# First block's norm, transposes and logits one step later, and the second group's tile numbers loaded behind a second layer's products

## The chip, the cores and the metric

The kernel runs on one core of a Trainium2 chip. The metric is the device time of one execution in microseconds; three runs of the kernel before have a median of 201.23 us (200.9 to 202.34). The engines are TensorE (PE, with its weight loads as PEld), VectorE (DVE), ScalarE (ACT), GpSimd (POOL) and SyncE (SP), which here only issues transfers. Each engine takes its instructions in order, and they wait for one another through semaphores.

## The reference

The input is 8 sequences of 256 tokens with 128 features. Two mixtures of experts run one after the other, and their result is added to the input.

```python
# stage 1, per sequence: two of eight experts, chosen from cond_8, and a shared one (inner width 512)
w, sel = top_k(softmax(cond), 2); w = w / w.sum()
c = sum_e w_e * ((gelu(x @ g_e) * (x @ u_e)) @ d_e) + (gelu(x @ sg) * (x @ su)) @ sd
# stage 2, per token: one of eight experts, and a shared one (inner width 256), weights rounded to three levels
h = layernorm(c) * gamma + beta
probs = softmax(h @ router_w.T)
ffn = silu(h @ sw1.T) @ sw2.T + max(probs) * (silu(h @ ew1[argmax].T) @ ew2[argmax].T)
out = x + ffn
```

## The kernel before

**Stage 1** is a loop over steps. A step is one sequence, one expert and one half of its inner width. The 16 shared steps come first, then 32 steps for the chosen experts, numbered (i, q) with i from 0 to 3 and q from 0 to 7: two sequences for each i, four steps for each sequence. In a step TensorE makes the gate product and the up product (`gate_up`, lines 446 to 448, 12 matmuls of 256 columns, since 16-bit high and low parts stand for 32-bit values), and the down product of the step three before (`down`, lines 473 to 475, 6 matmuls). ACT makes the gelu (line 728) and the high part of the product of the step before (`act_part_hi`, line 734); DVE makes the product (line 906) and its low part (line 912). There are two banks for gate and up each, so the gate/up product of a step waits until gelu and product of two steps earlier are done.

**Between the steps** the preparation of stage 2 is interleaved, at places that tables name by (i, q). For a block of four tiles of 128 tokens (two sequences) it runs: `to_tokens` (TensorE transposes the result of stage 1 into the bank ps_a, line 493), `statistics` (DVE), `deviation` (POOL, lines 1281 and 1283, gives `rstd` and `shift`), `normalise` (ACT, line 774, reads ps_a and writes `norm`), `to_features` (TensorE transposes `norm` into the bank ps_b, line 500), `features` (ACT, line 781), `logits` (TensorE, line 507, into ps_b) and `choose` (DVE, lines 993 to 1002, reads ps_b). The tables are TOKENS_AT, NORM_AT, FEATURES_AT and LOGITS_AT; the first entry of each is that of the first block. `abs_sums(f)` (ACT, lines 761 and 763) and POOL's `round_first` round the first-layer weights of expert f; `round_second` does it on DVE for the second layer, and `second_weights(k)` transposes two of these on TensorE (line 519) into ps_b, from where ACT copies them (line 769). A wait guards each use of ps_a and ps_b. Within a step TensorE does `gate_up`, then what the tables put there, then `down`. ACT does gelu, the high part of the step before, `abs_sums`, `second_weights`, `normalise`, `features`, in this order.

**Stage 2** has units: three shared ones, eight tile units (TU[0] to TU[7], of 3 or 4 tiles of tokens that a scatter through device memory has sorted by expert; four for the first group of tokens, four for the second), one shared and four dense ones. For each unit TensorE makes the first layer (`first_layer`, lines 624, 630, 639), ACT the silu (lines 836 to 846), TensorE the second layer (`second_layer`, line 664), and DVE takes the result. The loop runs first_layer(u), sorted_T for unit u + 2 (transposes of its sorted tokens, line 594), second_layer(u - 1). The weights of a tile unit are addressed by registers of TensorE's sequencer. `experts_of(g)` (line 601) waits for the table of group g and loads its tile numbers into these registers, 15 for group 0 and 13 for group 1, with one TENSOR_LOAD. Group 1 is needed from TU[4] on.

## Time and profile before

| | |
|---|---|
| median of three runs | 201.23 us |
| the profiled execution | 203.34 us, of which the span from first to last instruction 201.6 us |
| busy: PE, DVE, ACT, POOL | 169.7, 136.8, 114.6, 86.3 us |
| mean granted clock of TensorE | 0.947 of 2.4 GHz |

Read the rows as follows. A timeline row has the start in us, the duration in us, the engine, the line of the kernel, the operation with its output and input, a count, and in brackets how long the engine had been idle before and who ended that. A merged row lasts from its first to its last instruction. A windows row has the stretch, its length, the engine's busy time in it with the number of instructions, the granted clock of TensorE as a share of 2.4 GHz, the busy share of the DMA engines and GB/s. A waits row names who waited for whom, with the total in us, how many times, and the longest. Durations in the view of one line are in ns. Matmuls are pipelined, so consecutive ones start closer together than one lasts.

### The profile page before, as it was taken

To read this page: it belongs to the slowest core of one execution; us is meant where nothing else is said; L and a number is where in the kernel's file an instruction comes from. 1 tells how busy PE (TensorE), PEld (TensorE's weight loads), DVE (VectorE), ACT (ScalarE), POOL (GpSimd) and SP (SyncE) were. 2 spreads that over 40 slices of the span, in tenths; PEclk is the share of its full clock that TensorE was granted. 3 is DMA by queue.
4 is the path that set the end of the run, shared out by engine and by line. 5 is a ranking of instruction groups with operands and counts; after the bars stand their busy time and mean duration, and the time that the engine had idled before them with its cause. 6 is when DMAs were issued, how large, how long until landed. Compare 5 with 4: busy or idle time off the path is not lost.

```text
span 201.6 us, 4484 instructions
## 1 busy us (share of the span) xinstructions
PE 169.7 (84%) x1375; PEld 144.9 (72%) x1375; DVE 136.8 (68%) x350; ACT 114.6 (57%) x281; POOL 86.3 (43%) x139
## 2 busy tenths in 40 slices
PE   0699799999999996799999999779755999379680
PEld 0377588888888995588888887458644999269580
DVE  0348999973799999547998986686761345721655
ACT  4329666465776863827794655755448387326330
POOL 5080000004999599244799477100750004724600
PEclk9999999999999999559999999999996699969998
DMA  3997669995000000000000001250126123313413
GB/s 110 304 338 244 184 190 298 302 340 153 16 13 18 13 7 18 7 13 5 7 10 13 16 26 54 69 142 0 42 63 197 37 72 107 93 39 91 129 45 104
DMA packets 26823, 19.80 MB, mean 98 GB/s; under 512 B 4713, under 2 KB 23537, under 8 KB 26801
## 3 DMA queue, kind: packets, MB, share of 16 engines
q1 hardware_dynamic: 25616, 17.38, 29.3%
q0 software_dynamic: 896, 1.84, 3.0%
q10 hardware_dynamic: 288, 0.30, 0.6%
q8 instruction: 13, 0.21, 0.4%
q14 instruction: 10, 0.07, 0.1%
HBM read 13.28 MB, written 5.64 MB: 94 GB/s over the span
## 4 chain that ended last, share of the span: by engine, by line
PE 57%; DVE 11%; issue 8%; ACT 7%; another core or an unknown queue 4%; SPq 4%; POOL 4%; DMA 3%; DVEq 0%; ACTq 0%; POOLq 0%
PE ps_gate L664 7%; PE ps_out L459 6%; PE ps_up L664 5%; PE ps_gate L446 3%; PE ps_up L446 3%; PE ps_gate L448 3%; PE ps_gate L447 3%; PE ps_up L447 3%; PE ps_up L448 3%; DMA region<-in_L_cond_skill_down 3%; DVE a L912 2%; PE ps_out L473 2%; PE ps_out L475 2%; PE ps_out L474 2%
## 5 line engine op out<-in xcount | busy, mean ns | idle before, releaser
L728 ACT ACTIVATE g_sb<-ps_gate 128x512 f32<-128x512 f32 x48 | 28.6, 595 | 30.4 <-PE ps_gate L448 26.6
L906 DVE SCALAR_TENSOR_TENSOR a_sb<-g_sb,mix_w,ps_up 128x512 f32<-128x512 f32 x32 | 23.9, 746 | 15.3 <-PE ps_up L448 9.4
L446 PE MATMUL ps_up<-x,w 128*128 128x256 f16 x96 | 26.9, 280 | 2.1 <-DVE a L906 1.5
L446 PE MATMUL ps_gate<-x,w 128*128 128x256 f16 x96 | 27.3, 285 | 1.6 <-DVE x L882 1.4
L447 PE MATMUL ps_gate<-x,w 128*128 128x256 f16 x96 | 27.3, 285 | 0.0
L448 PE MATMUL ps_gate<-x,w 128*128 128x256 f16 x96 | 27.2, 284 | 0.0
L447 PE MATMUL ps_up<-x,w 128*128 128x256 f16 x96 | 26.8, 280 | 0.0
L448 PE MATMUL ps_up<-x,w 128*128 128x256 f16 x96 | 26.8, 279 | 0.0
L1295 POOL DMA_INDIRECT routed<-routed_scratch,slot_u x14 | 13.3, 952 | 28.1 <-DMA routed_scratch<-w 24.4
L876 DVE SCALAR_TENSOR_TENSOR w<-region,w 128x512 f16<-128x512 f32 x26 | 17.4, 681 | 8.4 <-ACT w L712 6.0
L734 ACT ACTIVATE a<-a_sb 128x512 f16<-128x512 f32 x32 | 20.1, 627 | 4.4 <-DVE a_sb L906 4.4
L912 DVE TENSOR_TENSOR a<-a_sb,a 128x512 f16<-128x512 f32 x32 | 22.2, 694 | 0.0
L1248 POOL TENSOR_SCALAR scales<-sums 128x3 f32<-128x3 f32 x9 | 2.3, 260 | 45.0 <-ACT abs_junk L763 44.5
L1286 POOL DMA_INDIRECT sorted_scratch<-norm,slot_u x14 | 15.1, 1077 | 15.1 <-DVE slot_u L1032 11.6
L473 PE MATMUL ps_out<-a,w 128*128 128x256 f16 x64 | 18.0, 281 | 0.8 <-DVE a L912 0.8
L475 PE MATMUL ps_out<-a,w 128*128 128x256 f16 x64 | 18.0, 282 | 0.0
L474 PE MATMUL ps_out<-a,w 128*128 128x256 f16 x64 | 18.0, 282 | 0.0
L664 PE MATMUL ps_gate<-region 128*128 128x128 f32 (+1 forms) x116 | 17.2, 311 | 0.0
L846 ACT ACTIVATE region<-ps_gate,tile_scale 128x128 f32<-128x128 f32 x32 | 9.2, 376 | 13.8 <-PE ps_gate L639 8.4
L664 PEld LDWEIGHTS ps_gate<-region 128*128 128x128 f32 x116 | 16.6, 225 | 0.4
L664 PE MATMUL ps_up<-region 128*128 128x128 f32 (+1 forms) x124 | 16.0, 278 | 1.0 <-issue 0.8
L459 PE MATMUL ps_out<-a,w 128*128 128x256 f32 x64 | 16.5, 380 | 0.0
(150 smaller groups left out, 388.6 us busy)
## 6 DMA issues: line engine op xcount, KB each, us to landing
region<-in_L_cond_skill_gate SPq DMA_DIRECT2D x8, 256.0 KB, 4.1
region<-in_L_cond_skill_up SPq DMA_DIRECT2D x8, 256.0 KB, 4.5
region<-in_L_cond_skill_down SPq DMA_DIRECT2D x8, 256.0 KB, 5.2
x_tok<-in_x SPq DMA_DIRECT2D x4, 256.0 KB, 6.3
f_raw<-in_L_ffn_expert_w SPq DMA_DIRECT2D x1, 1024.0 KB, 11.3
routed_scratch<-w SPq DMA_DIRECT2D x4, 256.0 KB, 2.6
sorted_scratch<-zeros SPq DMA_DIRECT2D x1, 960.0 KB, 10.6
sorted_scratch<-zeros SPq DMA_DIRECT2D x1, 832.0 KB, 11.2
```

The costliest lines, as they stand in the source:

```text
L446: pe.matmul(dst, w16[:, w_cols(e, 0, col)], x16[:, 0, xs], start=True, stop=False)
L447: pe.matmul(dst, w16[:, w_cols(e, 0, col)], x16[:, 1, xs], start=False, stop=False)
L448: last = pe.matmul(dst, w16[:, w_cols(e, 1, col)], x16[:, 0, xs], start=False, stop=True)
L459: last = pe.matmul(ps_out[batch % 2][:, 0:S], sd_32[Q % 2][:, m * P:(m + 1) * P], a32[:, Q % 4, m * S:(m + 1) * S], start=first and m == 0 ...
L473: pe.matmul(dst, w16[:, w_cols(e, 0, col)], hi, start=first and m == 0, stop=False)
L474: pe.matmul(dst, w16[:, w_cols(e, 0, col)], lo, start=False, stop=False)
L475: last = pe.matmul(dst, w16[:, w_cols(e, 1, col)], hi, start=False, stop=final and m == 1)
L664: last = pe.matmul(ps_y[u % 2][:, t * P:(t + 1) * P], s, w, start=c == 0, stop=c == FC - 1)
L728: act.activation(g_sb[:, Q % 2, :], ps_gate[Q % 2][:, :], ACT.Gelu_apprx_tanh, scale=1.0 / WS).then_inc(gelu_done, 1)
L734: act.activation(a16[:, Q % 4, 0, :], a_sb[:, Q % 2, :], ACT.Copy).then_inc(ahi_done, 1)
L906: dve.scalar_tensor_tensor(out=dst, in0=g_sb[:, Q % 2, :], scalar=weight, in1=ps_up[Q % 2][:, :], op0=ALU.mult, op1=ALU.mult).then_inc(pro ...
L912: dve.tensor_tensor(a16[:, Q % 4, 1, :], a_sb[:, Q % 2, :], a16[:, Q % 4, 0, :], ALU.subtract).then_inc(alo_done, 1)
```

## The change

The first block's `normalise` goes from (1, 6) to (1, 7), its `to_features` and `features` from (1, 7) to (2, 0), its `logits` and `choose` from (2, 0) to (2, 1). The transposes of `second_weights(1)` in (2, 2) go to the bank ps_a instead of ps_b; they wait for the first `norm` and no longer for `choose`, and `to_tokens(1)`, the next to write ps_a, now waits for ACT's copy out of it. `second_weights(2)`, in ps_b, waits for `choose` in exchange. In stage 2 `experts_of(1)` moves within the turn of u = TU[2] from ahead of sorted_T and second_layer(TU[1]) to behind them.

```diff
-    NORM_AT = [(1, 6), (2, 5), (3, 5)]
-    FEATURES_AT = [(1, 7), (2, 6), (3, 6)]
-    LOGITS_AT = [(2, 0), (2, 7), (3, 7)]
+    NORM_AT = [(1, 7), (2, 5), (3, 5)]
+    FEATURES_AT = [(2, 0), (2, 6), (3, 6)]
+    LOGITS_AT = [(2, 1), (2, 7), (3, 7)]
...
                 if part >= 1:
                     pe.wait_ge(norm_done, part)
+                if part == 1:
+                    pe.wait_ge(w2_done, 2)
...
                 if (i, q) == (2, 2):
-                    second_weights(1, ps_b, ldif_done, 1)
+                    second_weights(1, ps_a, norm_done, 1)
                 if (i, q) == (2, 4):
-                    second_weights(2, ps_b, w2_done, 2)
+                    second_weights(2, ps_b, ldif_done, 1)
...
                 if u == TU[0]:
                     to_tokens(4)
-                if u == TU[2]:
-                    experts_of(1)
                 if u == TU[3]:
                     to_features(4, slots_ready, 2)
...
                 if u > TU[0]:
                     second_layer(u - 1)
+                if u == TU[2]:
+                    experts_of(1)
...
                 if (i, q) == (2, 2):
-                    second_weights(1, ps_b)
+                    second_weights(1, ps_a)
```

TensorE behind the gate/up product of (1, 7), before. The two ISA rows prepare the addresses of the next expert; ps_out is the down product.

```order
L448 MATMUL ps_up<-x,w 128x256
L538 TENSOR_LOAD top_i
L538 ISA x2
L500 MATMUL ps_b<-ident,norm 128x128 x4
L473 ISA
L473 MATMUL ps_out<-a,w 128x256
L474 MATMUL ps_out<-a,w 128x256
```

And at the same place in the changed kernel, whose line numbers are two higher from there on:

```order
L448 MATMUL ps_up<-x,w 128x256
L540 TENSOR_LOAD top_i
L540 ISA x2
L473 ISA
L473 MATMUL ps_out<-a,w 128x256
L474 MATMUL ps_out<-a,w 128x256
```

The four transposes of `norm` are gone from there; they stand one step later, behind the gate/up product of (2, 0).

ACT from the gelu of (1, 6) to the gelu of (2, 0), before (g_sb is the gelu, a the high part, abs_junk the sums):

```order
L728 ACTIVATE g_sb<-ps_gate 128x512
L734 ACTIVATE a<-a_sb 128x512
L774 ACTIVATE norm<-ps_a,shift,rstd 128x128 x4
L728 ACTIVATE g_sb<-ps_gate 128x512
L734 ACTIVATE a<-a_sb 128x512
L761 ACTIVATE abs_junk,sums<-f_raw 128x128 x2
L763 ACTIVATE abs_junk,sums<-f_raw 128x256
L781 ACTIVATE h_all<-ps_b,beta_sb,gamma_sb 128x512
L728 ACTIVATE g_sb<-ps_gate 128x512
```

And now:

```order
L730 ACTIVATE g_sb<-ps_gate 128x512
L736 ACTIVATE a<-a_sb 128x512
L730 ACTIVATE g_sb<-ps_gate 128x512
L736 ACTIVATE a<-a_sb 128x512
L763 ACTIVATE abs_junk,sums<-f_raw 128x128 x2
L765 ACTIVATE abs_junk,sums<-f_raw 128x256
L776 ACTIVATE norm<-ps_a,shift,rstd 128x128 x4
L730 ACTIVATE g_sb<-ps_gate 128x512
L736 ACTIVATE a<-a_sb 128x512
L783 ACTIVATE h_all<-ps_b,beta_sb,gamma_sb 128x512
```

`norm` has moved behind a gelu, a high part and the three sums.

TensorE in the turn of TU[2] before, from the last products of its first layer (ps_up) to the first of second_layer(TU[1]) (ps_gate, line 664):

```order
L639 MATMUL ps_up<-region 128x128 x2
L601 TENSOR_LOAD tile_e
L594 MATMUL ps_out<-ident,w 128x128 x4
L664 ISA
L664 MATMUL ps_gate<-region 128x128
```

And now, from the transposes on, and behind a line of "..." the end of second_layer(TU[1]) with the first layer of TU[3]:

```order
L641 MATMUL ps_up<-region 128x128 x2
L596 MATMUL ps_out<-ident,w 128x128 x4
L666 ISA
L666 MATMUL ps_gate<-region 128x128
...
L666 MATMUL ps_gate<-region 128x128
L603 TENSOR_LOAD tile_e
L641 ISA
L641 MATMUL ps_gate<-region 128x128 x2
```

The load has moved past the four transposes and the eight products of second_layer(TU[1]), each of which has a register operation (ISA) of its own.

## Rows read from the trace of the kernel before

**Rows 1.** The page, span in 40 slices: TensorE's busy tenths, its granted clock.

```profile
PE   0699799999999996799999999779755999379680
...
PEclk9999999999999999559999999999996699969998
```

**Rows 2.** The waits: engine, line, waited for; total us, times, longest.

```profile
PE ps_b L500 <- ACT norm L774: 3.0, 1, 3.0
```

**Rows 3.** Timeline of TensorE, the last products before its wait and the transposes.

```profile
76.71 0.27 PE L473 MATMUL ps_out<-a,w 128*128 128x256 f16 x1
...
77.37 0.27 PE L446 MATMUL ps_gate<-x,w 128*128 128x256 f16 x1
...
78.88 0.27 PE L448 MATMUL ps_up<-x,w 128*128 128x256 f16 x1
82.11 1.11 PE L500 MATMUL ps_b<-ident,norm 128*128 128x128 f32 x4 [2.96 <-ACT norm L774]
```

**Rows 4.** Windows of TensorE, behind the wait.

```profile
core 0: us, PE busy (x), PEclk, DMA share, GB/s
...
82.11:91.32 9.21, 9.21 (x44) 0.50 0.04 7
91.32:103.00 11.68, 11.68 (x108) 1.00 0.04 8
```

**Rows 5.** Timeline of ACT around `norm`.

```profile
78.22 0.63 ACT L734 ACTIVATE a<-a_sb 128x512 f16<-128x512 f32 x1 [1.37 <-DVE a_sb L906]
80.56 1.50 ACT L774 ACTIVATE norm<-ps_a,shift,rstd 128x128 f32<-128x128 f32 x4 [1.70 <-POOL shift L1283]
81.94 0.61 ACT L728 ACTIVATE g_sb<-ps_gate 128x512 f32<-128x512 f32 x1
...
82.94 0.33 ACT L761 ACTIVATE abs_junk<-f_raw 128x128 f16<-128x128 f32 x1
...
83.92 0.79 ACT L781 ACTIVATE h_all<-ps_b,beta_sb,gamma_sb 128x512 f32<-128x512 f32 x1
```

**Rows 6.** Timeline of POOL and of DVE around the same steps.

```profile
79.98 0.54 POOL L1283 TENSOR_TENSOR shift<-neg_mean,rstd 128x4 f32<-128x4 f32 x1
...
79.11 0.75 DVE L906 SCALAR_TENSOR_TENSOR a_sb<-g_sb,mix_w,ps_up 128x512 f32<-128x512 f32 x1
...
88.61 0.19 DVE L993 TENSOR_REDUCE lmax<-ps_b 128x4 f32<-128x32 f32 x1
...
92.04 0.75 DVE L906 SCALAR_TENSOR_TENSOR a_sb<-g_sb,mix_w,ps_up 128x512 f32<-128x512 f32 x1 [2.34 <-PE ps_up L448]
...
100.05 0.74 DVE L906 SCALAR_TENSOR_TENSOR a_sb<-g_sb,mix_w,ps_up 128x512 f32<-128x512 f32 x1
```

**Rows 7.** Timeline of TensorE from unit 2's first layer to unit 3's.

```profile
151.94 0.67 PE L639 MATMUL ps_up<-region 128*128 128x128 f16 x8 [0.24 <-ACT region L846]
154.52 1.09 PE L594 MATMUL ps_out<-ident,w 128*128 128x128 f32 x4 [1.91 <-issue]
...
158.81 0.99 PE L639 MATMUL ps_gate<-region 128*128 128x128 f16 x8
```

**Rows 8.** Lines 601 and 664: durations in ns, first and last start.

```profile
L601 PEldq TENSOR_LOAD <-tile_e x1: 1601/1601/1601, 138.2 to 138.2; - x1
...
L601 PEldq TENSOR_LOAD <-tile_e x1: 2007/2007/2007, 152.3 to 152.3; - x1
...
L664 PE MATMUL ps_up<-region x16: 269/275/361, 146.5 to 149.4; 128*128 x16
L664 PEldq FUSED_REGOPS  x8: 42/44/51, 146.2 to 147.1; - x8
```

**Rows 9.** Windows of TensorE behind the load and around a later idle time.

```profile
154.50:159.50 5.00, 4.98 (x27) 0.50 0.11 32
...
189.60:191.70 2.10, 0.01 (x2) 1.00 0.83 246
```

**Rows 10.** Issue of the second group's sorted tiles; the landing of the largest.

```profile
149.60 1.97 SPq L400 DMA_DIRECT2D w<-sorted_scratch  x4
...
w<-sorted_scratch SPq DMA_DIRECT2D x1, 256.0 KB, 2.7
```

## The prediction

> **What bounds the kernel now.** I read the 40 slices first [rows 1]. TensorE is busy nearly throughout from slice 4 to slice 24, and the clock row dips in three places: slices 17 and 18 (80.6 to 90.7 us, since a slice is 5.04 us), 31 and 32, and 36. The one gap of TensorE in its dense part stands at the first dip, in slices 16 and 17. The waits list names one long wait of TensorE for another engine in the middle part: 3.0 us for ACT's `norm` [rows 2]. The timeline of TensorE shows where: the last product of step (1, 7) starts at 78.88 and lasts 0.27, so it ends at 79.15, and the transposes of `norm` into ps_b begin at 82.11 after 2.96 us idle [rows 3]. Before the wait six products take 0.66 us (76.71 to 77.37), so a step of 18 takes 1.97 us. Behind the wait TensorE is busy without a gap, but at a granted 0.50, which is the level of 1.2 GHz, from 82.11 to 91.32; from 91.32 it runs at 1.00, 2.4 GHz, again [rows 4]. That wait therefore costs twice: 2.96 us idle, and 9.21 us of work that takes double its time, so 4.6 us.
>
> Who is late there? ACT. Its queue is in order [rows 5]: the copy of step (1, 5) at 78.22, then `norm` from 80.56 (it had waited 1.70 us for POOL's `shift`, which ends at 79.98 + 0.54 = 80.52 [rows 6]), then only at 81.94 the gelu of step (1, 7).
>
> In the late part the same is seen with another cause [rows 7]. The first layer of tile unit 2 ends at 151.94 + 0.67 = 152.61; the next transposes start at 154.52 after 1.91 us "issue". A TENSOR_LOAD of `tile_e` starts at 152.3 and takes 2.007 us [rows 8], so it ends at 154.31, just before. Behind it the clock is at 0.50 from 154.5 to 159.5 [rows 9], and the first layer of unit 3 starts at 158.81.
>
> **Part 1: norm, transposes and logits one step later.** No instruction is added or removed. What moves is the point at which TensorE needs `norm`: one down product and one gate/up product, 1.97 us of work, now stand ahead of it. But ACT's `norm` moves too. Its queue, worked out from durations of before: gelu of (1, 7) at about 78.7 to 79.3 (its input is ready at 78.2). The copy of (1, 6) waits for DVE's product, 79.11 + 0.75 = 79.86 [rows 6], so 79.9 to 80.5. Then come the sums, which stood behind `norm` and stand ahead of it now: 82.94 to 83.92 in the trace, 0.98 us, so to 81.4. `shift` is ready at 80.5, so POOL is no longer waited for. `norm` takes 1.50: 81.4 to 82.9. TensorE starts the transposes at 82.95, 0.84 later than before, having done 1.97 more by then. Gain: 1.97 - 0.84 = **1.1 us**; the idle time shrinks from 2.96 to about 1.8, and does not vanish. I take 1.1; the bounds are 0.2 (ACT another 0.9 late, the length of a gelu and its gap) and 2.0 (all 1.97, if ACT keeps its old time).
>
> **The clock behind it.** The 4.6 us come back if the shorter idle time leaves the clock up. This decides more than the wait itself, and the trace has rows on both sides. 2.96 us idle brought it down. 2.09 us idle at 189.6 did not: the granted clock stays 1.00 there [rows 9]. Against that, the 1.91 at 152.61 has 0.50 behind it [rows 9], though it came right after other short gaps such as the 0.24 before 151.94 [rows 7]. So 1.8 us is below the 2.09 that left the clock up, but the length alone doesn't settle it. Bounds: 0 (no fall) and 4.6 (the same 9.2 us at half). Nearest to 2.09 is 0; one fall of some 2.4 us of lost work in about half the executions makes 1.2. I take back **-4.6 + 1.2 = -3.4 us**.
>
> The Trainium skill, page "TensorE: Matmul & The Clock Gate", section "Terms", prices time at the low clock as that time times one minus the ratio; from the fall at about 81 to 91.32 that is 5.1 us. The rows give 4.6, since TensorE had nothing to do in the first microsecond of it; by the page the sum would be 0.5 lower, and the rows decide.
>
> **What else moves with part 1.** `choose`, five small DVE instructions of 0.19 us with short gaps, about 1.1 us (the first at 88.61 [rows 6]), goes from (2, 0) to (2, 1), where a round_second stands too. In the trace DVE works from the product of (2, 1) at 92.04 to the next one behind the statistics of (2, 3) at 100.05 with hardly a gap, 8.0 us [rows 6]; with `choose` in it that becomes 9.1, against three steps of TensorE (5.9 us) and the short passes between them. So DVE falls behind there by more than a microsecond. But it has slack: the product of (2, 3) is only needed by the up product of (2, 5), two steps or 3.9 us later. I cost it at nothing; without that slack it is the 1.1 us of `choose`. The second weights use ps_a in (2, 2), so they don't wait for `choose`. In exchange the tokens of (2, 3) wait for ACT's copy out of ps_a; ACT makes it behind the gelu and the copy of (2, 2), while TensorE has a down product and a whole gate/up product (1.97 us) to do first, so over 1 us is left. The wait costs nothing with that cover, and what ACT is late without it. The sums of f = 6 start at 80.4 instead of 82.94, which only helps POOL. Everything from there to 150 us is a chain that starts from these products; no transfer in it is tied to a fixed time, so the gain is carried along.
>
> **Part 2: the load of tile numbers behind second-layer products.** The load itself stays 2.0 us (bounds 1.6 and 2.0, the two in the trace [rows 8]). What changes is what covers it. The first load starts at 138.2, and TensorE goes on with products without idle time: the sequencer had run ahead of the array. For the second layer of tile unit 0, whose weights have computed addresses, the eight register operations run from 146.2 to 147.1, while the last of its 16 passes (8 products of 32 bits, two passes each) starts at 149.4 [rows 8]. So after the change: transposes from 152.61 (their tiles landed 2.7 us after the first issue, at 149.60 + 2.7 = 152.3 [rows 10]), register operations to about 153.4, load to 155.4, next layer 0.2 later, as in the trace, at 155.6. The transposes and the 16 passes themselves take 158.81 - 154.52 = 4.3 us at the clock of this trace, so up to 156.9; the load is hidden. Gain: 158.81 - 156.9 = **1.9 us**, exactly the idle time. With the clock up the work would end at 154.8 and the load at 155.6 would decide, 3.2 us earlier than 158.81. If the sequencer cannot run ahead, the load follows the products: 156.9 + 2.2 = 159.1, a loss of 0.3. I take 1.9, as the row of the first load is the nearest.
>
> The Trainium skill, page "Runtime: NRT & Kernel Launch", section "Instruction fetch mechanics", gives about 200 ns a register for such a load. The 13 numbers would make it 2.6 us, an estimate; the trace has 2.007, and 1.601 for 15. By the page, with the clock up, the next layer would start at 156.2 and not at 155.6; the sum at this trace's clock stays as it is.
>
> **The sum.** The profiled execution took 203.34 us (span 201.6). 203.3 - 1.1 - 3.4 - 1.9 = **196.9 us**. The median of three runs was 201.23, 2.1 less. I don't take these 2.1 off again, because what varies between executions is most likely the length at half clock, and the sum already removes most of it.
>
> **Rivals.**
> - *The clock falls all the same and stays low as long.* For it: 1.8 us of idle time remains, and in the trace the clock stayed at 0.50 for nine microseconds although TensorE was busy all the while [rows 4]. Against: the 2.09 us that left the clock up. Then 203.3 - 1.1 - 1.9 = 200.3. Chance 0.16.
> - *Both places keep the clock up.* 203.3 - 1.1 - 4.6 - 3.2 = 194.4. For it: both idle times shrink. Against: TensorE still waits for ACT just ahead of the second place [rows 7], and the edit leaves that as it is. Chance 0.14.
> - *The load isn't hidden*, the second edit does nothing: 196.9 + 1.9 + 0.3 = 199.1. Against: the first load. Chance 0.07.
> - *Slower: a new wait at the tokens of (2, 3).* TensorE now waits there for ACT's copy out of ps_a, with the down product and everything else queued behind. It decides from the point where ACT is over 1.3 us later than worked out. A stall of the size of the old one (3.0) with its half clock (4.6) would come on top of the first rival's 200.3 less what it still gains: 200.3 + 3.0 + 4.6 = 207.9; a short one of 1 us with the 4.6 gives 205.9. For it: ACT already sets the pace at (1, 7). Against: a gelu and its copy take ACT 1.0 us (81.94 to 82.94 [rows 5]), half a step, so with one set of sums (0.98) and one more copy in (2, 1) and (2, 2) it still has less to do than TensorE. Chance 0.04.
> - Forecast: 0.59.
>
> The range reaches from 194.2 to 200.4: the rival with the clock up, the one with the clock down, and what lies between. About 1% is what a measurement of this kernel can tell from no change, so faster means below 199.2: the forecast, the second rival, half of the third and a part of the first, 0.83; within 1%: 0.13; slower: 0.04.
>
> **What would show it.** In the changed kernel's profile: TensorE's idle time before the transposes of `norm` 1.8 us and not 3.0, at about 81 to 83; ACT's `norm` behind the sums, not behind POOL; granted clock 1.00 from 84 to 92, or a stretch at 0.50 that is shorter than 9.2 us; no idle time of TensorE between the first layer of unit 2 and the transposes, the TENSOR_LOAD at about 153.4 minus the shift, and at most 0.8 us idle behind the 16 passes. The forecast is wrong if the clock row shows the same two long dips, if a wait at the tokens of (2, 3) or one for DVE's products appears, or if the waits of ACT after 170 us take back what came before.

## The result: 195.5 us instead of 202.3, with the profile after

Measured side by side on one chip, the changed kernel takes a median of 195.48 us (five executions, 194.8 to 198.25) and the kernel before 202.34 us (five executions, 200.9 to 202.89, the three shown ahead of the prediction among them). The ratio is 0.968, with a 95% interval of 0.963 to 0.973. The forecast was 196.9, with a range of 194.2 to 200.4. All ratios in this document compare fast executions only, those within 1.5% of the fastest of the same kernel, and the record counts both profiled executions as slow, so their traces are of executions longer than the medians.

The profiled execution of the changed kernel took 198.25 us, the longest of its five, with a span of 196.4 us and a mean granted clock of 0.963. Before it was 203.34 us, a span of 201.6 and 0.947. So the traces show 5.1 us of gain, and the medians 6.9.

The page of the changed kernel, the span in 40 slices of 4.91 us: TensorE's busy tenths and its granted clock, to be laid beside [rows 1].

```profile
PE   0697799999999999699999999779759995699490
PEclk9999999999999999999999999999996999669879
```

Slices are counted from 1, as in the prediction. The first dip is gone: slices 1 to 30 all have a 9. The second has shrunk from two slices to one (slice 31). Of the last 45 us it shows more dips than before and not fewer: slices 35 and 36 read 6 where one did (36 of before), and slices 38 and 39 read 8 and 7.

The timeline of TensorE in the changed kernel around the first place, which answers to [rows 3]: start, duration, engine, line, operation, and in brackets the idle time before it with what ended it.

```profile
79.53 0.28 PE L473 MATMUL ps_out<-a,w 128*128 128x256 f16 x1 [0.51 <-issue]
...
82.81 0.66 PE L502 MATMUL ps_b<-ident,norm 128*128 128x128 f32 x4 [1.14 <-ACT norm L776]
...
85.27 0.96 PE L509 MATMUL ps_b<-routerT,h_all 128*128 128x8 f32 x8
...
91.09 0.66 PE L495 MATMUL ps_a<-ident,c_sb 128*128 128x128 f32 x4 [0.49 <-DVE c_sb L963]
```

The transposes of `norm` start at 82.81, hardly later than the 82.11 of before, but with a whole step more done ahead of them. They take 0.66 us and not 1.11, because the clock is up. The tokens of (2, 3) start at 91.09; before they started at 96.27. So 5.2 us are gained within fourteen. The row of before:

```profile
96.27 0.66 PE L493 MATMUL ps_a<-ident,c_sb 128*128 128x128 f32 x4
```

The 0.51 us ahead of the down product at 79.53 belong to a load too. TensorE's sequencer loads the next expert number (`top_i`, line 540) and prepares its addresses from 78.6 to 79.2. Before, the same operations ran from 78.8 to 79.4, under the wait for `norm`; now a product stands behind them.

Windows of TensorE in the changed kernel, the first two behind the first place, as [rows 4]; the third behind the first layer of tile unit 2 and the fourth near the end, as [rows 9]: busy time and instructions, granted clock, DMA share, GB/s.

```profile
core 0: us, PE busy (x), PEclk, DMA share, GB/s
82.81:92.00 9.19, 8.70 (x78) 1.00 0.05 10
92.00:103.00 11.00, 11.00 (x102) 1.00 0.05 10
147.70:151.00 3.30, 3.30 (x17) 0.50 0.63 181
185.20:188.60 3.40, 3.31 (x16) 0.50 0.38 121
```

Behind the transposes the clock now stays at 1.00; before it was 0.50 for 9.21 us. At the second place it is still 0.50, for 3.3 us of busy time instead of five. The last row is new: near the end there is a stretch at 0.50 where before the clock held.

The timeline of TensorE in the changed kernel from tile unit 2 to unit 3, as [rows 7], and then near the end:

```profile
143.61 0.27 PE L666 MATMUL ps_up<-region 128*128 x1 [0.47 <-issue]
...
145.92 0.69 PE L641 MATMUL ps_gate<-region 128*128 128x128 f16 x8 [1.22 <-ACT region L848]
146.85 0.67 PE L641 MATMUL ps_up<-region 128*128 128x128 f16 x8 [0.24 <-ACT region L848]
147.37 0.88 PE L596 MATMUL ps_out<-ident,w 128*128 128x128 f32 x4
148.04 3.40 PE L666 MATMUL ps_gate<-region 128*128 x16
151.28 0.61 PE L641 MATMUL ps_gate<-region 128*128 128x128 f16 x8
...
183.96 0.60 PE L632 MATMUL ps_gate<-region 128*128 128x256 f16 x4 [1.81 <-ACT region L842]
185.29 1.03 PE L632 MATMUL ps_up<-region 128*128 128x256 f16 x4 [0.73 <-ACT region L842]
186.12 3.15 PE L666 MATMUL ps_gate<-region 128*128 128x128 f32 x16
189.10 1.95 PE L666 MATMUL ps_up<-region 128*128 128x128 f32 x16
```

The row for the transposes (147.37) has no bracket: TensorE has nothing to wait for between the first layer of unit 2 and them, where before there were 1.91 us. The load of tile numbers now lies under the sixteen passes of line 666, as the row of that load says (durations in ns, first and last start):

```profile
L603 PEldq TENSOR_LOAD <-tile_e x1: 1338/1338/1338, 148.5 to 148.5; - x1
```

It starts at 148.5 and ends at 149.8, while the passes run to 151.4.

The clock at this place needs a closer look, since [rows 9] begin only behind the idle time. The window within it, in the trace of the kernel before:

```profile
152.75:154.50 1.75, 0.00 (x0) 0.50 0.81 233
```

So before, the clock was down 0.15 us after the 1.91 us of idle time had begun at 152.61. The idle time at the load can't be what brought it down. It fell 0.8 us behind the start of the same product in both traces: 152.75 against 151.94 before, 147.7 against 146.85 after. Both have the same short idle times of TensorE just ahead (0.38, 0.46, 1.21 and 0.24 us before; 0.47, 0.46, 1.22 and 0.24 after).

Three starts of the same instructions say where the time went. Unit 2's first layer, second half: 151.94 before and 146.85 after, so 5.1 us from the first place. The dense first layer behind the tile units, and the last second layer, in the trace of the kernel before:

```profile
180.96 0.60 PE L630 MATMUL ps_gate<-region 128*128 128x256 f16 x4 [1.34 <-ACT region L836]
...
194.21 2.02 PE L664 MATMUL ps_up<-region 128*128 128x128 f32 x16
```

The first of them is at 173.14 after: 7.8 us earlier. Of these, 2.4 arose between unit 2's first layer and unit 3's (6.87 us from start to start before, 4.43 after). The second is at 189.10 after (the last row of the fence further up), so 5.1 us again: in the profiled execution the end gave 2.7 us back. From the one to the other TensorE was busy for 13.42 us after and 11.04 before, at a mean granted clock of 0.84 and 1.00, so 2.4 of the 2.7 are lost through the clock, and 0.3 as idle time. A stretch at 0.50 that began at about 168.2, behind an idle time of 2.94 us before 167.69 that the trace calls issue (2.18 before), reaches into this part, and a second one starts at 185.2, behind two waits for ACT. ACT in turn had waited 4.04 us for something that the trace puts down to no engine (the timeline of ACT in the changed kernel):

```profile
182.97 0.84 ACT L842 ACTIVATE region<-ps_gate,scales 128x256 f32<-128x256 f32 x2 [4.04 <-remote]
184.40 0.84 ACT L842 ACTIVATE region<-ps_up,scales 128x256 f32<-128x256 f32 x2 [0.58 <-remote]
```

The other four executions took 194.8 to 195.54, about 3 us less than the profiled one. Their mean granted clock was 0.973 to 0.988, above the 0.963 of the profiled one, so at least part of what was lost at the end is this execution's own. They have no trace that would show where.

### The profile page after: what moved, and what is told of

The parts are those of the page before. It is cut to its first block, busy times and chain, and to the rows that moved or that the text cites. A ratio compares the mean times of both kernels' runs of the same rounds, so it can differ in the third digit from the quotient of the medians.

```text
span 196.4 us, 4484 instructions
## 1 busy us (share of the span) xinstructions
PE 166.4 (85%) x1375; PEld 142.9 (73%) x1375; DVE 137.1 (70%) x350; ACT 114.6 (58%) x281; POOL 85.9 (44%) x139
## 4 chain that ended last, share of the span: by engine, by line
PE 50%; DVE 18%; ACT 10%; issue 7%; another core or an unknown queue 6%; SPq 4%; DMA 3%; DVEq 0%; ACTq 0%
PE ps_gate L666 7%; PE ps_out L459 6%; PE ps_up L666 5%; DVE a L914 5%; DMA region<-in_L_cond_skill_down 3%; PE ps_up L446 3%; PE ps_gate L446 3%; PE ps_up L448 3%; PE ps_gate L448 3%; PE ps_up L447 3%; PE ps_gate L447 3%; ACT region L848 2%; PE ps_up L641 2%; DVE a_sb L908 2%
## 5 line engine op out<-in xcount | busy, mean ns | idle before, releaser
L446 PE MATMUL ps_gate<-x,w 128*128 128x256 f16 x96 | 26.4, 275 | 2.3 <-DVE x L884 1.4
L446 PE MATMUL ps_up<-x,w 128*128 128x256 f16 x96 | 26.5, 276 | 1.7 <-DVE a L908 1.5
L447 PE MATMUL ps_up<-x,w 128*128 128x256 f16 x96 | 26.5, 276 | 0.0
L448 PE MATMUL ps_up<-x,w 128*128 128x256 f16 x96 | 26.5, 276 | 0.0
L448 PE MATMUL ps_gate<-x,w 128*128 128x256 f16 x96 | 26.5, 276 | 0.0
L447 PE MATMUL ps_gate<-x,w 128*128 128x256 f16 x96 | 26.5, 276 | 0.0
L473 PE MATMUL ps_out<-a,w 128*128 128x256 f16 x64 | 17.5, 273 | 1.4 <-DVE a L914 0.8
L666 PEld LDWEIGHTS ps_gate<-region 128*128 128x128 f32 x116 | 17.9, 240 | 0.6 <-issue 0.3
L666 PE MATMUL ps_gate<-region 128*128 128x128 f32 (+1 forms) x116 | 18.2, 323 | 0.0
L475 PE MATMUL ps_out<-a,w 128*128 128x256 f16 x64 | 17.4, 272 | 0.0
L474 PE MATMUL ps_out<-a,w 128*128 128x256 f16 x64 | 17.4, 272 | 0.0
```

What stands on the lines that cost most here:

```text
L446: pe.matmul(dst, w16[:, w_cols(e, 0, col)], x16[:, 0, xs], start=True, stop=False)
L447: pe.matmul(dst, w16[:, w_cols(e, 0, col)], x16[:, 1, xs], start=False, stop=False)
L448: last = pe.matmul(dst, w16[:, w_cols(e, 1, col)], x16[:, 0, xs], start=False, stop=True)
L473: pe.matmul(dst, w16[:, w_cols(e, 0, col)], hi, start=first and m == 0, stop=False)
L474: pe.matmul(dst, w16[:, w_cols(e, 0, col)], lo, start=False, stop=False)
L475: last = pe.matmul(dst, w16[:, w_cols(e, 1, col)], hi, start=False, stop=final and m == 1)
```

## The experiments

The experiments ran on two chips, numbered 10 and 12 in the record, which has no number for the chip of the comparison above. The kernel before takes a median of 188.6 to 188.8 us on these two, and 202.3 there, so I take that one for another (the first chip, from here on). Every comparison below is with runs of the kernel before on the same chip, and differences of the changed part are read from the traces at the same instructions. Two things differ there and matter. The waits of ACT and TensorE behind 145 us that are put down to no engine are absent. And at the turn of tile unit 2 TensorE waits about 4 us for its sorted tiles from memory, so the load of tile numbers has a cover already. The transfer isn't slower there. In `e2_part2` TensorE is done with the first layer of unit 2 at 144.85 instead of 152.61, 7.8 us earlier than on the first chip, and the transfer is issued at 145.83 instead of 149.60, only 3.8 us earlier; it lands after 3.0 us, against 2.7.

Two theories stood against each other for the 5 us at the first place. Theory A: the wait for `norm` costs twice, and mostly through the clock; shortening the idle time keeps the clock up. Theory B: the order of instructions itself is what counts (ACT's queue, the sums ahead of `norm`), and the clock follows other things. For the second place: the load was the cause of the 1.91 us, or it was not.

**One part at a time.** `e1_part1` has the tables and the bank swap of the change, but `experts_of(1)` ahead as before; `e2_part2` is the kernel before with `experts_of(1)` behind the second layer.

```diff
 # e1_part1, against the changed kernel
+                if u == TU[2]:
+                    experts_of(1)
                 if u == TU[3]:
                     to_features(4, slots_ready, 2)
...
                     second_layer(u - 1)
-                if u == TU[2]:
-                    experts_of(1)
 # e2_part2, against the kernel before: the same lines moved the other way
```

> Only the first part (norm, transposes and logits one step later, second weights in ps_a), the load of tile numbers where it was. My theory (half the gain is TensorE's clock behind the first wait): 1.1 us of idle time and 2.8 to 4.6 us of half clock go, so 4 to 5.5 us under the kernel before, about 197.5, with the stretch at 0.50 near 82 to 91 gone from the trace and the idle time of 1.9 us at the load still there. Rival (the wait only costs its idle time, the clock is noise): 1.1 us under, about 201.

> Only the second part (the load of tile numbers behind the second layer). My theory (the load is hidden by the products): 1.9 us under the kernel before, about 200.3, with the wait for norm and its half clock still there. Rival (the load still follows the products, or the late waits of ACT take it back): within 0.5 us of before. If the clock comes back earlier too, up to 3.

Measured: `e1_part1` 185.17 us (184.86 to 186.81), ratio 0.986 (0.979 to 0.993); `e2_part2` 189.14 us (187.24 to 191.27), ratio 1.008 (1.003 to 1.013), with 188.81 for the kernel before. Part 1 alone brings 3.6 us in the medians and 1.4% (2.7 us) by the ratio, less than the 4 to 5.5 expected. Part 2 alone brings nothing, or costs a little; the 1.9 us expected of it aren't there, and its rival had that. The timeline of TensorE in `e1_part1`, where the load is not moved:

```profile
82.85 0.66 PE L502 MATMUL ps_b<-ident,norm 128*128 128x128 f32 x4 [1.22 <-ACT norm L776]
...
146.14 1.12 PE L596 MATMUL ps_out<-ident,w 128*128 128x128 f32 x4 [4.06 <-DMA w<-sorted_scratch]
```

The wait for `norm` is 1.22 us, as in the changed kernel (1.14). At the turn of unit 2 the sorted tiles come 4 us after TensorE is ready for them, so the load ahead of them is hidden under that wait. On this chip there is nothing for part 2 to win. `e2_part2` keeps the whole stall of before, and its windows (columns as further up) show the clock behind it:

```profile
82.06 0.66 PE L500 MATMUL ps_b<-ident,norm 128*128 128x128 f32 x4 [2.97 <-ACT norm L774]
...
93.43 0.66 PE L493 MATMUL ps_a<-ident,c_sb 128*128 128x128 f32 x4
```

```profile
82.06:83.20 1.14, 1.14 (x10) 0.97 0.00 0
83.20:86.60 3.40, 3.40 (x19) 0.51 0.00 0
86.60:92.00 5.40, 5.40 (x52) 1.00 0.08 17
```

The idle time is the same to 0.01 us as in [rows 3], but the time at 0.50 is 3.4 us and not 9.21. If everything took double its time there, the same wait would cost 1.7 us through the clock in one execution and 4.6 in another; what starts of instructions show is told with the next experiment.

**The idle time filled.** `e3_fill` is the kernel before with 24 matmuls of no use put into the idle time ahead of the transposes. Their result is overwritten. If it is the clock that costs (A), the order being untouched, most of the clock's share comes back.

```diff
+                if (i, q) == (1, 7):
+                    pe.wait_ge(w2_done, 1)
+                    for _ in range(24):
+                        pe.matmul(ps_b[:, 0:S], w16[:, w_cols(SH, 0, 0)], x16[:, 0, 0:S], start=True, stop=True)
                 if (i, q) in FEATURES_AT:
```

> The kernel before, with 24 extra matmuls (256 columns, results overwritten, nothing left out) in TensorE's queue between the gate/up product of (1, 7) and the transposes that wait for norm: 2.6 us of filler in an idle time of 2.96. The wait lasts as long as before, only the clock can differ. Clock theory: granted clock 1.00 up to the second layer, 3 to 4.6 us under before, about 198.5. Rival (idle time is what costs): no change, 202.3; if the filler runs past the wait, slower.

Measured: 187.37 us (186.06 to 187.88), with 188.81 for the kernel before: 1.4 us less in the medians, where 3 to 4.6 were expected. The ratio is 1.005 (1.000 to 1.010), which says no difference. What the filler does is read in its trace:

```profile
79.45 2.79 PE L578 MATMUL ps_b<-x,w 128*128 128x256 f16 x24 [0.29 <-issue]
82.11 0.66 PE L500 MATMUL ps_b<-ident,norm 128*128 128x128 f32 x4
...
92.12 0.66 PE L493 MATMUL ps_a<-ident,c_sb 128*128 128x128 f32 x4
```

```profile
79.45:82.10 2.65, 2.65 (x24) 1.00 0.14 28
82.10:92.00 9.90, 9.88 (x90) 1.00 0.04 9
```

The transposes start at 82.11, at the very time of before, so not a single product comes earlier. Yet the clock stays at 1.00 behind them. The tokens of (2, 3) start at 92.12, against 93.43 in `e2_part2` and 96.27 in the trace of the kernel before: the clock is worth 1.3 and 4.2 us up to there, somewhat less than half of 3.4 and 9.21. On TensorE the ranks of block 0 start at 104.77 in `e3_fill`, at 106.10 in `e2_part2` (3.4 us at 0.50) and at 108.47 in the trace of the kernel before (9.2 us at 0.50). The order on ACT and TensorE is the same in all three, but for the filler. It is the idle time that brings the clock down here, and the clock is worth 1.3 and 3.7 us of these starts. The changed kernel has 103.30, so its order is worth another 1.5 us.

The mean granted clock, which is on record for each execution, says the same of those without a trace. Of the kernel before, 28 of the 44 executions side by side with the experiments are below 0.97, and of `e2_part2`, which keeps the wait, 8 of 12. Of `e3_fill` it is none of 12, and none of 23 of the kernels with part 1 (`e1_part1`, `f0_changed`, `g3_changed`, `g2_part1`, `e5_all_psb`). At an equal mean clock, 0.980 to 0.987, the kernel before takes 186.6 us on average (8 executions), `e3_fill` 186.7 (4) and the kernels with part 1 185.0 (10). At 0.974 to 0.978 they take 187.5 (5), 187.8 (6) and 186.3 (7). So the filler is worth nothing except through the clock. Part 1 is worth 1.2 to 1.6 us besides the clock, and the rest of its 3.6 us in the medians comes from the clock being low less often or for less time. Above 0.987 there are only two executions of the kernel before (184.56 and 185.98), too few to compare.

**Which step gets ahead of which.** `e4_norm_stays` is the changed kernel with `norm` left at (1, 6): only the transposes and the logits move. If ACT's order costs anything, this should be faster than the changed kernel.

```diff
-    NORM_AT = [(1, 7), (2, 5), (3, 5)]
+    NORM_AT = [(1, 6), (2, 5), (3, 5)]
```

> The changed kernel, but ACT's norm of the first block back at (1, 6), ahead of a gelu, a high part and the three sums; transposes at (2, 0) and logits at (2, 1) as changed. By my working ACT's order sets the remaining wait of 1.1 us: norm is ready 0.84 us earlier, the idle time at (2, 0) falls to about 0.3 or 0.9, and the kernel is 0.5 to 0.9 us faster than the changed one, about 194.8. Rival (gelu and product of (1, 7) come late then and hold the up product of (2, 1)): same or slower.

Measured: 186.98 us (185.62 to 187.94), ratio 0.993 (0.989 to 0.997). It is 1.8 us below the kernel before in the medians and 1.8 above `e1_part1`, so slower than the changed order, and not 0.5 to 0.9 us faster as expected. (`e1_part1` has the load in its old place, which `g2_part1` and `g3_changed` below show to make no difference there. In the traces the ranks of block 0 start 1.1 us later than in `e1_part1`.) Rows of `e4_norm_stays` on TensorE and on ACT:

```profile
82.12 0.66 PE L502 MATMUL ps_b<-ident,norm 128*128 128x128 f32 x4 [0.38 <-ACT norm L776]
85.77 1.06 PE L509 MATMUL ps_b<-routerT,h_all 128*128 128x8 f32 x8 [1.03 <-ACT h_all L783]
```

```profile
80.57 1.50 ACT L776 ACTIVATE norm<-ps_a,shift,rstd 128x128 f32<-128x128 f32 x4 [1.70 <-POOL shift L1285]
...
84.93 0.79 ACT L783 ACTIVATE h_all<-ps_b,beta_sb,gamma_sb 128x512 f32<-128x512 f32 x1
```

`norm` is ready earlier and the wait for it is 0.38 us, but ACT again stands 1.70 us for POOL, as in [rows 5], with the gelus and the copies behind it. It is then late for `h_all`, and TensorE waits 1.03 us for that. The wait moved one step on. Moving `norm` as well is part of the gain: it fills ACT's wait for POOL with work.

**One step further.** `e6_one_more` moves the transposes and the logits of the first block once more, to (2, 1) and (2, 2).

```diff
-    FEATURES_AT = [(2, 0), (2, 6), (3, 6)]
-    LOGITS_AT = [(2, 1), (2, 7), (3, 7)]
+    FEATURES_AT = [(2, 1), (2, 6), (3, 6)]
+    LOGITS_AT = [(2, 2), (2, 7), (3, 7)]
```

> The changed kernel with transposes and features of the first block yet one step later, at (2, 1), logits and choose at (2, 2), norm still at (1, 7). By my working norm is ready at about 82.8 while TensorE gets to (2, 1) at about 83.4, so the remaining wait of 1.1 to 1.2 us is gone altogether: 1.1 us under the changed kernel, and choose stands behind the take_batch for which TensorE waited 0.5 us at the tokens of (2, 3), so up to 1.6. Rival (DVE's queue, with choose, take_batch, split and statistics in two steps, becomes the bound): within 0.5 us of the changed kernel.

Measured: 184.83 us (184.63 to 185.56), ratio 0.982 (0.974 to 0.990), beside 186.02 us (185.22 to 186.55), ratio 0.987 (0.978 to 0.995), for the unmodified changed kernel beside it, `f0_changed`. The kernel before has 188.74 there.

> The changed kernel as it is, beside the others of this call. If the chip shows the unexplained waits of ACT and TensorE behind 145 us, the second edit counts (about 1.9 us) and it is 5 to 6.5 us under before. If they are missing, TensorE waits about 4 us for the sorted tiles at the turn of TU[2] in any case, the load was hidden there already, and only the first edit counts: 3 to 4 us under before.

The wait at the first block is gone, and a new one stands at the second block (TensorE and ACT of `e6_one_more`):

```profile
84.02 0.63 PE L502 MATMUL ps_b<-ident,norm 128*128 128x128 f32 x4 [0.24 <-issue]
97.90 0.66 PE L502 MATMUL ps_b<-ident,norm 128*128 128x128 f32 x4 [1.30 <-ACT norm L776]
```

```profile
96.34 1.51 ACT L776 ACTIVATE norm<-ps_a,shift,rstd 128x128 f32<-128x128 f32 x4 [0.18 <-POOL shift L1285]
```

In `f0_changed` the two waits are 1.22 and 0.24 us. TensorE itself is well ahead in `e6_one_more`: it begins the tokens of (2, 3) at 89.66 without a wait, in `f0_changed` at 91.12 after 0.27 us. But the norm of the second block comes out of DVE's statistics, then POOL's `shift`, then ACT, and DVE has no gap from the product at 84.92 on. It makes the last of these statistics, `neg_mean`, at 94.69 (`e6_one_more`) and at 95.14 (`f0_changed`), only 0.45 us apart. So 1.0 of TensorE's 1.46 us went into the new wait, and the ranks of block 0 start at 103.14 instead of 103.59, 0.45 us earlier. The pace here is set by DVE. That is what the rival said; the theory had 1.1 to 1.6 us. (The medians are 1.2 us apart, more than this place explains; four executions each.)

**The bank swap.** `e5_all_psb` is the whole change, but with the second weights of the first two blocks left in ps_b as before, and without the new wait of the tokens.

```diff
-                if part == 1:
-                    pe.wait_ge(w2_done, 2)
...
-                    second_weights(1, ps_a, norm_done, 1)
+                    second_weights(1, ps_b, ldif_done, 1)
...
-                    second_weights(2, ps_b, ldif_done, 1)
+                    second_weights(2, ps_b, w2_done, 2)
```

> The changed kernel with the second weights of (2, 2) back in the bank ps_b, so that they wait for choose again, and without the wait of the tokens for ACT's copy. In the changed kernel's trace choose has read ps_b about 0.7 us before these transposes start (its second instruction ends at 87.3, the transposes start at 88.04), so the bank was free in any case: no difference, within 0.3 us of the changed kernel. Rival (DVE is late enough to hold them, and everything behind): 0.5 to 1 us slower.

> The changed kernel, to compare with the part alone and with the load ahead on the same chip. 3 to 4 us under the kernel before where the sorted tiles are waited for, 5 to 6.5 where they are in time.

> Only the first part again, beside the changed kernel in the same call, which the first time were not on one chip. Where TensorE waits 4 us for the sorted tiles: equal to the changed kernel within 0.5 us. Where it doesn't: 1.9 to 2.4 us slower than the changed kernel.

Measured side by side on chip 10, with 188.64 us for the kernel before: `e5_all_psb` 184.96 us (184.88 to 185.92), ratio 0.985 (0.976 to 0.995); the unmodified changed kernel `g3_changed` 185.20 us (184.82 to 186.46), 0.989 (0.979 to 0.999); part 1 alone again, `g2_part1`, 185.09 us (184.97 to 185.42), 0.987 (0.977 to 0.996). The three can't be told apart. In `e5_all_psb`:

```profile
88.06 0.60 PE L519 MATMUL ps_b<-ident,f_raw 128*128 128x128 f32 x4
91.10 0.66 PE L493 MATMUL ps_a<-ident,c_sb 128*128 128x128 f32 x4 [0.47 <-DVE c_sb L961]
```

The second weights' transposes start without a wait at 88.06 in either bank (88.04 in the changed kernel), and the tokens wait 0.47 us for DVE (0.49 in the changed kernel). So the swap neither gains nor costs, and the 0.5 us at the tokens is not its wait for ACT: it is DVE's `c_sb`, behind the choice of experts. `e6_one_more` bears this out: with `choose` moved behind `c_sb`, the tokens start without a wait. And since `g2_part1` is level with `g3_changed`, part 1 is the whole gain on this chip.

**The wait for sorted tiles.** At the turn of unit 2 the transposes of sorted tiles are queued ahead of a second layer that doesn't need them. `f3_sorted_last` puts them behind it.

```diff
-                if u in TU and u + 2 in TU:
+                if u in TU and u + 2 in TU and u != TU[2]:
                     sorted_T(TU.index(u + 2))
                 if u > TU[0]:
                     second_layer(u - 1)
                 if u == TU[2]:
                     experts_of(1)
+                    sorted_T(TU.index(u + 2))
```

> The changed kernel with sorted_T of TU[4] behind second_layer(TU[1]) and the load, instead of ahead of them. Theory (where the tiles arrive late, the second layer queues behind a transfer that it doesn't need): on a chip with the 4 us wait for the sorted tiles, 16 passes (1.8 us, up to 3.4 at half clock) and the load go into that wait, so 1.8 to 3 us under the changed kernel. On a chip where the tiles are there in time: no change. Rival (the load then stands in front of the transposes, exposed): up to 1 us slower.

Measured: 182.43 us (181.57 to 183.9), ratio 0.972 (0.962 to 0.982). TensorE and the windows of `f0_changed`:

```profile
146.82 1.12 PE L596 MATMUL ps_out<-ident,w 128*128 128x128 f32 x4 [4.48 <-DMA w<-sorted_scratch]
147.73 3.62 PE L666 MATMUL ps_gate<-region 128*128 x16
151.14 0.80 PE L641 MATMUL ps_gate<-region 128*128 128x128 f16 x8
```

```profile
146.80:151.10 4.30, 4.28 (x20) 0.50 0.53 147
```

and of `f3_sorted_last`:

```profile
141.81 2.00 PE L666 MATMUL ps_gate<-region 128*128 x16
145.87 0.66 PE L596 MATMUL ps_out<-ident,w 128*128 128x128 f32 x4 [2.05 <-DMA w<-sorted_scratch]
146.36 0.61 PE L641 MATMUL ps_gate<-region 128*128 128x128 f16 x8
```

```profile
145.87:150.00 4.13, 4.13 (x49) 1.00 0.74 210
```

The sixteen passes took 3.62 us at half clock behind a 4.48 us wait, and take 2.00 at full clock inside it. What remains of the wait is 2.05 us, and the clock doesn't fall behind it. Unit 3's first layer starts at 146.36 instead of 151.14, 4.8 us earlier; the medians are 3.6 us apart, above the 1.8 to 3 expected. To see whether the place of the load matters, `g1_load_first` has the same edit with the load ahead of the second layer.

```diff
 # against f3_sorted_last
+                if u == TU[2]:
+                    experts_of(1)
                 if u > TU[0]:
                     second_layer(u - 1)
                 if u == TU[2]:
-                    experts_of(1)
                     sorted_T(TU.index(u + 2))
```

> The kernel with sorted_T of TU[4] last (which was 3.6 us under the changed one), but the load of tile numbers put back ahead of second_layer(TU[1]). If moving the second layer into the wait for the sorted tiles made that gain, this is equal to it, since the load (1.1 to 1.6 us) still ends before the tiles land: again about 3.6 us under the changed kernel, 182.4. If the place of the load made it, 1 to 2 us are lost. On a chip where the tiles are in time, the load is exposed and this is 1 to 2 us slower than the changed kernel.

Measured: 182.24 us (181.48 to 182.59), ratio 0.970 (0.960 to 0.979), on chip 10 beside `g3_changed` with 185.20, so 3.0 us under the changed kernel. `f3_sorted_last` has 182.43 and a ratio of 0.972, but on chip 12; the two weren't measured side by side. TensorE in `g1_load_first`:

```profile
143.04 2.05 PE L666 MATMUL ps_gate<-region 128*128 x16 [0.76 <-DVE w L1087]
146.81 0.66 PE L596 MATMUL ps_out<-ident,w 128*128 128x128 f32 x4 [1.72 <-DMA w<-sorted_scratch]
```

The second layer starts 1.2 us later (143.04 instead of 141.81), 1.0 of it through the load, since the first layer ahead of it was 0.2 us later already. But the load uses up wait time only: the tiles still arrive later. So no worth of the load's place can be seen in this version, and the place of the transposes is worth 3.6 us on one chip and 3.0 on the other.

**Both together.** `f4_best` is `e6_one_more` and `f3_sorted_last` in one.

> Both of the above together. Theory: they lie in different stretches and add up, 1.1 to 4 us under the changed kernel. Rival: the first block's gain is swallowed by a later wait for a transfer (POOL's scatters, the sorted tiles), so no better than the reordered second layer alone.

Measured: 182.12 us (181.21 to 183.06), ratio 0.966 (0.957 to 0.976). It beats both kernels on that chip, by 6.6 us (188.74) and 3.9 us (186.02), but it can't be told from `f3_sorted_last` (0.3 us). The simpler `f3_sorted_last` is what I would keep. Whether it gains as much on the chip of the first comparison was not measured. There the tiles came on time: the transposes of the changed kernel had no wait at all.

## Why the prediction was right, point by point

- **The wait for `norm`: right.** Forecast: transposes at 82.95, gain 1.1. Measured 82.81, with 1.97 us more work done ahead, so 1.97 - 0.70 = 1.27 us. The idle time was 1.14 and not 1.8 us right before them, because TensorE had already lost 0.51 us ahead of the down product at 79.53; the two make 1.65. These 0.51 us are the load of `top_i`, which the working left out; it costs nothing as long as `norm` is what TensorE waits for in the end. ACT's order came as worked out: the sums, then `norm` at 81.27 (forecast 81.4), with no wait for POOL.
- **The clock behind it: mechanism right, term too small for the pair of traces.** I took back 3.4 of 4.6 us, as a mean over executions with and without a fall. In the trace after, the clock didn't fall at all. From the step to the tokens of (2, 3) 5.18 us were gained; less 1.27, and with the 0.49 below added, 4.4 us are left for the clock (4.2 by `e3_fill`). In all eight profiles that have this wait at 1.14 to 1.22 us (the changed kernel three times, `e1_part1`, `g2_part1`, `e5_all_psb`, `f3_sorted_last`, `g1_load_first`), the clock row has nothing but nines there. `e3_fill` shows it by itself: no product earlier, clock at 1.00. What I had not expected is that behind the same 2.96 us the clock was low for only 3.4 us in `e2_part2`, worth 1.3 us. On the chips of the experiments this term is smaller, and so is the gain (2.7 and 3.4 us in the medians of the changed kernel, 1.3 and 1.1% by the ratios). How often the clock was low for nine microseconds in the kernel before on the first chip, one trace can't say.
- **The cost of `choose` at (2, 1): nothing forecast, 0.49 us measured.** I looked at the up product of (2, 5) as the one that needs DVE. The first to wait was another, the tokens of (2, 3), for `c_sb`, which DVE makes from the down product. The slack I counted was that of the wrong reader. `e5_all_psb` has 0.47 us with the banks as before, so the swap is not its cause.
- **Bank swap and the wait of the tokens for ACT: right.** Nothing gained, nothing lost (`e5_all_psb` against `g3_changed`, 184.96 and 185.20). The slower rival, a new stall at the tokens, named the right place and the wrong engine, and its 0.49 us are half of the smallest stall that it was priced with.
- **The load: right in the trace, alone not shown.** Forecast 1.9 us with the clock still low; the interval from unit 2 to unit 3 shrank by 2.44, of which 1.91 is the idle time that is gone. The other 0.5 us are clock: the transposes began with it still up, where before all of this stood at 0.50. My reading of the clock there was wrong. I took the half-clock stretch to stand behind the 1.91 us, and counted them as an idle time that brings the clock down; it fell 0.15 us into them, and at the same place without them. So the end of this idle time was no reason for the second rival, in which the clock stays up at both places. The load itself took 1.34 us, below both my bounds (1.6 and 2.0), which changed nothing, as it lay under the passes. The load ran under the passes as forecast, so the sequencer does run ahead. But no experiment repeats this: on the other chips the load was covered by the wait for a transfer, and moving it changed nothing. That this edit was worth 2.4 us on the first chip rests on its two traces alone.
- **Everything is carried to the end: wrong in the profiled execution.** The sum assumed no new loss behind 150 us. By 173 us the trace had gained 7.8 us, more than the 6.4 of the sum, and then 2.7 went back through ACT's wait of 4.04 us and a clock at 0.50 for 3.4 us. That was named as what could go wrong (waits of ACT after 170 us), but had no price. The median, 195.48, is 2.8 us below the profiled time, and near what the trace up to 173 us would give (203.34 - 7.8 = 195.5).
- **The sum** of 196.9 was 1.4 above the median. By the traces the terms up to 173 us are 1.3 (forecast 1.1) for the wait, 4.4 (3.4) for the clock, -0.5 (0) for DVE and 2.4 (1.9) for the load, with 0.2 more behind that: 7.8 against 6.4. So the sum was 1.4 us too cautious by the traces, mostly on the clock, and the end of the profiled execution hid that. That the traced terms lead right to the median is partly luck: the sum starts from the profiled 203.34, 1.0 above the median of the kernel before. By the medians alone the gain is 6.9, against 6.4 forecast.
- **The signs of being wrong.** Two of those that I had listed did appear, both smaller than they were priced or feared: a wait at the tokens of (2, 3), for a result of DVE (0.49 us), and waits of ACT after 170 us that took back part of the gain (2.7 us, in the profiled execution). The first means that the working of DVE's slack failed, though its 0.5 us are small beside the range.

What stays open is the late waits of ACT (2.3, 3.2 and 3.9 us in both traces of the first chip, 4.04 in the one after) and TensorE's idle times called issue (2.2 and 2.9 us). They stand in both kernels' traces there and not in those of the other chips, and they stand where most of the difference of 188.6 and 202.3 us arises: the changed kernel reaches unit 2's first layer 5.1 us later there than in `f0_changed` (146.85 and 141.74), and takes 6.5 us longer from there to the end. No experiment reached them, since none ran on that chip.

## What to carry to other kernels

Price an idle time of TensorE at its own length plus the half-clock stretch behind it, and give that second part a range (1.3 and 4.2 us behind the same 2.96 us here); shortening the idle time can be enough, it need not vanish. Before you blame an idle time for a low clock, check how the clock stood as it began, and what came just ahead. When a step moves, list every reader of every engine it is queued on, the nearest first: the 0.5 us were lost at the reader that stood one place ahead of the one I checked. And look for waits on a transfer that stand ahead of work which doesn't need it: two lines moved brought about as much again as the whole change had on those chips (3.6 and 3.0 us, after 2.7 and 3.4).

## What the runs showed of the hardware

- Behind the same idle time the clock stays low for different times. 2.96 us idle gave 9.21 us at 0.50 [rows 4], and 2.97 us gave 3.4 us in `e2_part2`. Idle times of 1.14 to 1.22, 1.72 and 2.05 us (`g1_load_first`, `f3_sorted_last`) left it at 1.00, 4.48 us (`f0_changed`) did not. The length of one idle time doesn't decide alone, though. In the trace after, the clock fell at 147.7 with no idle time over 1.22 us ahead of it, but with several short ones close together (0.47, 0.46, 1.22 and 0.24 us from 143 to 147). It fell at 185.2 too, with 1.81 and 0.73 us of idle time just ahead. Nor does it fall at a fixed point of the idle time: in the trace before it was down at 81.1, 1.9 us into the 2.96, and in `e2_part2` at 83.1, 1.1 us after TensorE had gone back to work. The Trainium skill, page "TensorE: Matmul & The Clock Gate", section "Terms", prices time at the low clock as that time times one minus the ratio. That gives 1.7 us for `e2_part2` and 4.6 for the kernel before, estimates; against `e3_fill`, at the tokens of (2, 3), it was 1.3 and 4.2, somewhat less, and the measurement decides. The time at the low clock, behind one and the same wait, differs by a factor of 2.7.
- The load of 13 tile numbers took 2.007 us before, 1.338 in the trace after and 1.106 to 1.262 in the twelve traces of the experiments, though the instruction is the same; 15 numbers took 1.59 to 1.60 in all fourteen. The Trainium skill, page "Runtime: NRT & Kernel Launch", section "Instruction fetch mechanics", gives about 200 ns a register. That would be 2.6 us for the 13, an estimate; the longest here is 2.007, and the measurements decide.
- The same kernel takes 202.3 us on one chip and 188.6 to 188.8 on others, with equal times up to the first dip (`norm`'s transposes at 82.11 and 82.06). The difference arises behind it, in the clock and in waits that the traces put down to no engine. A gain in microseconds measured on one chip (6.9) is not the gain on another (2.7 and 3.4).
